# Three moves in the order of work of a fused vision and text block: the attention copy, the left-over copy and the gating transposes

## What is computed

```python
h = concat([patches(x) @ w.T + b, txt], axis=1)          # 32 x 273 x 128
# attention: 8 heads of 16; w_pre mixes the logits of the heads, w_post their weights
logits = einsum('bhij,gh->bgij', rope(q) @ rope(k).T * scale, w_pre)
attn = einsum('bhij,gh->bgij', softmax(logits), w_post)
h = h + (attn @ v) @ w_out.T + b_out                      # on layernorm(h)
# experts: top 2 of 8 by the gating logits
xn = layer_norm(layernorm(h)); p = softmax(xn @ Wg); top_p, top_i = top_k(p, 2)
o = gelu(xn @ W1[e] + b1[e]) @ W2[e] + b2[e]
h = h + layer_norm(x + sum(conf * o[top_i]))
```

## Time and profile before

| | |
|---|---|
| median of 3 runs | 1679.19 us (1678.18 to 1682.19) |
| the profiled execution | 1685.3 us, its span 1683.5 us |
| mean granted TensorE clock | 0.916 of full |
| busy: TensorE, VectorE, ScalarE, GpSimd | 79%, 66%, 62%, 52% of the span |
| first phase, from the first embedding to the last `proj` | about 34 to 1232 us of the span |

### The profile page before, as it was taken

The page is one execution under the profiler, slowest core; times in us unless marked ns, Lnnn a source line. Parts: engine busy times, 40 slices in busy tenths (PEclk is TensorE's granted clock), DMA queues, the critical chain, the costliest instruction groups (busy, mean ns, idle before and its releaser), DMA issues.

```text
span 1683.5 us, 37357 instructions
## 1 busy us (share of the span) xinstructions
PE 1325.3 (79%) x9026; PEld 1205.4 (72%) x9027; DVE 1104.7 (66%) x3669; ACT 1049.6 (62%) x3071; POOL 882.6 (52%) x1653
## 2 busy tenths in 40 slices
PE   1798888888888888888888888888837999999000
PEld 1687777777877777787777777777737999998000
DVE  1766677777667777766777776677624544544687
ACT  0476677777767777766777766677704555554566
POOL 1124444555544455554455554445543666666788
PEclk9799999999999999999999999999958999999555
DMA  5522343322334322333432232340003222221454
GB/s 145 97 35 40 42 59 52 44 41 45 45 47 55 51 40 42 45 44 51 55 48 41 42 46 43 53 54 19 18 19 91 77 79 72 79 73 45 142 157 135
DMA packets 110944, 101.35 MB, mean 60 GB/s; under 512 B 14171, under 2 KB 105278, under 8 KB 110324
## 3 DMA queue, kind: packets, MB, share of 16 engines
q1 hardware_dynamic: 98642, 75.75, 27.2%
q0 software_dynamic: 11328, 19.07, 3.8%
q10 hardware_dynamic: 866, 5.49, 0.9%
HBM read 70.60 MB, written 30.65 MB: 60 GB/s over the span
## 4 chain that ended last, share of the span: by engine, by line
PE 43%; DVE 22%; issue 15%; POOL 9%; ACT 6%; SPq 2%; DMA 2%; DVEq 2%; ACTq 0%; POOLq 0%
PE PS L1232 11%; PE PS L1471 8%; PE PS L1318 4%; DVE rounded L934 3%; DVE nmax L970 3%; PE PS L1458 2%; PE PS L1459 2%; PE PS L1460 2%; DVE VP L921 2%; ACT E L686 2%; DVE bst L876 2%; PE PS L1255 2%; POOL rs L638 2%; DVE sl L1029 2%; PE PS L1298 1%
## 5 line engine op out<-in xcount | busy, mean ns | idle before, releaser
L970 DVE TENSOR_REDUCE nmax<-PS 128x2 f32<-128x546 f32 (+1 forms) x288 | 206.2, 716 | 164.7 <-PE PS L1280 164.7
L1318 PE MATMUL PS<-AT,VP 128*128 128x273 f32 x1024 | 283.4, 399 | 0.0
L686 ACT ACTIVATE E<-PS,nmax 128x273 f32<-128x273 f32 x512 | 243.5, 482 | 36.0 <-DVE nmax L970 35.8
L1232 PE MATMUL PS<-wtok,arena 97*98 97x128 f32 x1024 | 195.5, 350 | 51.3 <-DMA arena<-in_x 34.3
L568 POOL DMA_INDIRECT dram_routed<-xr,slu x192 | 201.6, 1050 | 64.5 <-issue 64.5
L1232 PEld LDWEIGHTS PS<-wtok,arena 97*98 97x98 f32 x1024 | 182.5, 264 | 56.1 <-DMA arena<-in_x 34.0
L1278 PE MATMUL PS<-rounded 128*128 128x274 f32 (+1 forms) x576 | 215.3, 374 | 3.9 <-DVE rounded L939 2.9
L713 ACT COPY AT<-PS 128x512 f32<-128x512 f32 x256 | 151.3, 591 | 87.5 <-PE PS L1298 85.1
L619 POOL DMA_INDIRECT dram_results<-arena,du x152 | 166.0, 1092 | 64.2 <-issue 54.6
L1318 PEld LDWEIGHTS PS<-AT,VP 128*128 128x128 f32 x1024 | 180.2, 196 | 21.9
L1298 PE MATMUL PS<-small,E 128*128 128x128 f32 x1024 | 163.0, 283 | 39.3 <-ACT ATR L720 39.3
(11 more groups left out here) (195 smaller groups left out, 3296.7 us busy)
## 6 DMA issues: line engine op xcount, KB each, us to landing
arena<-in_x SPq DMA_DIRECT2D x96, 196.0 KB, 5.0
arena<-in_x SPq DMA_DIRECT2D x96, 189.0 KB, 8.4
arena<-dram_routed SPq DMA_DIRECT2D x76, 144.0 KB, 2.2
stage<-dram_results SPq DMA_DIRECT2D x32, 196.0 KB
dram_h<-H SPq DMA_DIRECT2D x32, 147.0 KB
w1hl<-dram_h SPq DMA_DIRECT2D x32, 147.0 KB
out<-w1hl SPq DMA_DIRECT2D x32, 98.0 KB
dram_routed<-xr,slu POOLq DMA_INDIRECT x192, 2.3
```

The lines of the kernel that those rows point to most:

```text
L686: nc.scalar.activation(bank, PS[0:rows, 2 * ((par + u) % 2) + t, 0:N], ACT.Exp, bias=nmax[0:rows, u, t:t + 1], accum_out=esum[0:rows, u, t ...
L970: v.tensor_reduce(nmax[0:rows, u], PS[0:rows, b0:b0 + 2, 0:N], AX.X, ALU.max, negate=True).then_inc(S["max"], 1)
L1232: last = mm(PS[0:R, MA, t * D:(t + 1) * D], xv[:, t * HP // 2:(t + 1) * HP // 2, :, q], wtok[:, q, :], start=(q == 0), stop=(q == QH - 1))
L1318: last = mm(acc, VP[:, par, g, c, :], AT[:, g, c, :], start=(g == 0 and c == 0), stop=False)
```

## The change

Three calls move; nothing is added or taken away.

```diff
--- before.py
+++ after.py
@@ -777,6 +777,8 @@
                     if u == 8 and has["emb"]:
                         k_hi(i + 1, 1 - par)
                     head = behind(i, u, 3, has)
+                    if u == 3 and has["res"]:
+                        attn_out(i - 1)
                     if head:
                         probsT(*head)
                     before = behind(i, u, 1, has)
@@ -785,16 +787,14 @@
                     lead = ahead_of(i, u, 3, has)
                     if lead and lead[1] > 0:
                         q_hi(lead[0], par if u + 3 < NU else 1 - par, lead[1] - 1)
+                    if head and head[1] in (HR, NH):
+                        restT(head[0], head[1] // HR - 1)
                     if has["attn"]:
                         exps(i, par, u)
-                    if head and head[1] in (HR, NH):
-                        restT(head[0], head[1] // HR - 1)
                     if u == 0 and has["rout"]:
                         xhat(i - 2, par)
                     if u == 1 and has["rout"]:
                         x2_T(i - 2)
-                    if u == 3 and has["res"]:
-                        attn_out(i - 1)
                     if u == 5 and has["rout"]:
                         act.wait_ge(S["logit_gap"], i - 1)
                         nc.scalar.activation(ed[:], dl[:], ACT.Exp).then_inc(S["gap_exp"], 1)
@@ -1411,8 +1411,6 @@
                         weighted_rest(last[0], lpar, last[1] // HR - 1)
                     if head and head[1] in (HR, NH):
                         rest_T(head[0], hpar, head[1] // HR - 1)
-                    if u == 1 and has["rout"]:
-                        x2T_(i - 2, par)
                     if u == 2 and has["rout"]:
                         gate(i - 2)
                     if emb:
@@ -1423,6 +1421,8 @@
                         if u in (6, 7):
                             qk(i + 1, u - 6, 0)
                             qk(i + 1, u - 6, 1)
+                    if u == 1 and has["rout"]:
+                        x2T_(i - 2, par)
                     if u == 4 and has["res"]:
                         proj(i - 1)
                     if u == 8 and has["rout"]:
```

## The result

| | before | changed |
|---|---|---|
| median | 1680.22 us (4 runs, 1678.18 to 1682.19) | 1698.16 us (4 runs, 1696.15 to 1699.84) |
| ratio | | 1.0103 (95%: 1.0090 to 1.0117) |
| profiled execution | 1685.3 us, span 1683.5 us | 1699.84 us, span 1698.0 us |
| images with a slow stretch, of 28 | 20 | 25 |
| mean distance from one first embedding half to the next | 36.66 us | 37.20 us |

The change costs 17.9 us by the medians (1698.16 - 1680.22), 14.5 us between the two profiled executions (that of before was 5 us above its median). The last two lines of the table are read from the starts of the first embedding halves of the 28 images in the middle of the first phase; an image counts as slow when the scores right behind that half run at the lower clock. The distance grew by 0.54 us, over 29 images 15.7 us: the loss lies in the first phase, spread over its images.

What follows compares the result with a forecast made beforehand. Bound by TensorE from the first embedding half to slot 3's scores, then by VectorE until VR. 6.4 + 0 + 0 + 0 + 2.9 = +9.3 us gave 1688.5 us; range 1670 to 1701, the forecast's own 1684 to 1696 us.

Steps and rivals of the forecast that it cites:

- the rival with every image slow: Longer TensorE idle piece costs all seven fast images their clock, GpSimd delayed too: +20.9, about 1700 us; chance 0.15.
- the clock term: Longer idle time before the first embedding half makes 2 of 7 fast images slow: +2.9 us (0 to +10.2).
- The gating transposes: Behind the first embedding half they cost TensorE their issue time, 0.22 us in 29 images: +6.4 us (5.8 to 11.6).
- The left-over copy, slot 7: Ahead of ScalarE's exponentials; keys rounded 0.26 us sooner, but GpSimd's list holds VectorE: 0 (-8.1 to +4.3).
- The left-over copy, slot 2: Waits for TensorE's left-over transposes and delays the exponentials under 1 us, covered by VectorE's 4.17 us idle time: 0.
- The attention copy: Head of slot 3: fits into ScalarE's wait; `proj` then waits for VectorE's L991 instead of the copy: 0.
- rival VectorE past HB: Slot 8: sooner keys let L1029 start before GpSimd's HB, saving 0.66 us an image; about 1663 us, chance 0.15.

Runs made afterwards that it cites:

- copies only: The changed kernel with the gating transposes back at their old place, so only the two ScalarE copies move: 1680.29 us, ratio 0.9999 against the kernel before.
- late HB: The kernel before with GpSimd's HB moved from the end of slot 8 to slot 1 of the next image: 1640.99 us; with both ScalarE copies moved too, 1656.82 us.
- the filled runs: Unread work in TensorE's idle time: changed kernel with matmuls 1663.19 us, with transposes 1663.63 us; ScalarE moves alone with matmuls 1659.21 us.
- the two sets: The changed kernel with a second, unread set of the three gating transposes at their old place in the wait: 1692.09 us, ratio 1.0082.

## Why the prediction was wrong

The direction was right, and so was the mechanism of the transposes; the forecast rise of 9.3 us was about half of the 17.9 us measured. The time lay inside the wide range only because that range had been drawn to hold the rival with every image slow: the forecast's own range, 1684 to 1696 us, missed the 1698.16 us. The step that failed is the clock term, +2.9 us, and beside it the transposes were priced too low. Point by point, in its own order:

- **The gating transposes**, +6.4 us: right in kind, small in size. I took 0.22 us from the lower end of 0.20 to 0.40 us; measured are 0.28 us on an image at full clock, 29 x 0.28 = +8.1 us. The 0.20 us in the earlier trace rows run from the start of three transposes to the scores behind them, and leave out that the transposes begin 0.17 us after the last matmul ahead of them, where the scores would have begun after 0.09 us.
- **The left-over copy, slot 7**, 0: right, and for the reason given: copies only is at 0.9999. VectorE's gain of 0.28 us became a wait for GpSimd's L558 and the held L1029. The runs with late HB show more than I had seen: even without HB there is no gain, because VectorE then waits 0.24 us for L558.
- **The left-over copy, slot 2**, 0: right; VectorE still waits up to 3.4 us for the scores of slot 3.
- **The attention copy**, 0: right; `proj` waits 1.4 us for L991.
- **The clock**, +2.9 us: this is the step that failed. I had looked at the idle time of one kind of image only; in the other it was 1.15 and 0.45 us, not 0.55 and 0.65 us. I let 2 of 7 fast images go slow, a guess between 0 and all. The count of slow images went from 20 to 25 of 28, and the price of the clock over 29 images from (36.66 - 35.64) x 29 = 29.6 us to (37.20 - 35.93) x 29 = 36.8 us, with the distances at full clock taken from the filled runs: +7.2 us. And I named the wrong cause, or at best the smaller one. I put it down to the longer, unbroken idle piece; the copies alone lengthen the idle time and change nothing, and in the two sets 3.7 us of clock and four of the six new slow images come with the transposes on the path, the idle time left as it was. The work added on the path cost nearly as much again through the clock (7.2 us on 8.1, of which half stands in the run with the two sets), and the prediction treated the two as separate.

8.1 + 7.2 = 15.3 us account for the 15.7 us of the distances; the ratio's interval allows 15.1 to 19.7 us. The rival nearest in time, every image slow, 1700 us, came near on the clock (25 images of 28) but reached its time with a third part, +4.3 us for a delayed GpSimd. L558 does take 0.47 us instead of 0.33 us, but nothing is lost by it beyond the gain of the sooner keys. Of the rival VectorE past HB nothing came: L1029 stayed behind HB in every image. VectorE, waiting for L558, has L1025 to do first, and HB starts 677.57 - (676.92 + 0.47) = 0.18 us after L558 has ended, ahead of L1029 at 677.71 us.

## What to carry to other kernels

Work that stood in a wait was free, and behind the wait it was on the path: before a call is moved past a wait, look whether the wait ends on something the call does not influence. Where TensorE's clock drops in some images, a few tenths on the path can cost half as much or as much again through the clock. Look for the engine that TensorE waits for rather than for TensorE's own order: half a microsecond less of waiting, or unread work in the wait, was worth more here than all three moves. VectorE, which got its input sooner, won nothing here, because 1.4 us further on it had to wait for GpSimd.

## What the runs showed of the hardware that was not expected

- Unread transposes in an idle piece kept TensorE's clock as well as unread matmuls: 1663.63 and 1663.19 us, no slow stretch in either.
- An operation of VectorE on 98x24 elements takes 0.76 us or more beside GpSimd's HB, and two of them take 0.28 us together without it; moving that one GpSimd instruction was worth 38 us in 1680, half directly and half through TensorE's clock.
- In five of the kernels the stretches at the lower clock follow each other after 37.55 or 71.68 us and after nothing else, whatever the length of an image; a kernel whose period comes close to 37.55 us has nearly all its images slow.
- The price of a slow stretch depends on where it begins. In the kernel before, two images of one kind whose stretches begin 1.38 and 2.71 us behind the start of the half take 36.99 and 37.46 us, against 35.86 us at full clock: 1.13 and 1.60 us. With the two sets the mean price was (36.95 - 35.93) x 28 / 23 = 1.24 us.
